# Causal attention of 16 heads: f32 matmuls replaced by three float32r products of split operands, with operands split on ScalarE, VectorE and GpSimd

## The chip, the cores and the metric

The kernel runs on one core of a Trainium2 chip. The metric is the device time of one execution in microseconds (us), measured without a profile; below it stands the time of before. The core has a matrix engine, TensorE (PE, with its weight loads shown apart as PEld), and VectorE (DVE), ScalarE (ACT), GpSimd (POOL) and SyncE (SP), which issues DMA. The engines run by themselves and meet at semaphores; each carries out its own instructions strictly in the order in which they are written.

## The reference

The program is a stack of 16 layers over one stream x of 1024 tokens with 256 features. The change is in one of them, the first attention of the third block ("L2a"):

```python
x = x + _L2_attn_a_ref(_layernorm(x, axis=-1), L2_attn_a_W_Q, L2_attn_a_W_K, L2_attn_a_W_V, L2_attn_a_W_O)

q = jnp.einsum('bsd,hed->bhse', x, W_Q)
scores = jnp.einsum('bhse,bhme->bhsm', q, k) * scale
scores = jnp.where(causal, jnp.float32(-1000000000.0), scores)
pattern = jax.nn.softmax(scores, axis=-1)
z = jnp.einsum('bhsm,bhme->bhse', pattern, v)
out = jnp.einsum('bhse,hde->bsd', z, W_O)
```

## The kernel before

All tensors of the layer are f32. `hT` holds the normalised x with features on the partitions. For each of the 16 heads `wide_attention` projects q and k (each [128, 1024], as two halves of 512 tokens: the items q0, k0, q1, k1) and v (items v0, v1), computes the scores of 8 tiles of 128 query rows, takes the row maximum, exponentiates, turns the probabilities with PE against an identity, multiplies by v, and projects with Wo into x.

The work is laid out by hand. A head has 8 slots s, one for each row tile, in the order `ROW_ORDER = (3, 7, 2, 6, 1, 5, 0, 4)`; row tile t sees t+1 key tiles, so the widths are 512, 1024, 384, 896, 256, 768, 128 and 640 columns. In slot s of head p, PE computes the scores of row s (`score`), then what `BESIDE[s]` lists, then the turn of the row before (`turn`). `BESIDE` places the six projections of head p+1 ("make0" to "make5") and, for head p-1, the products with v ("sum0", "sum1", for the lower and the upper 512 tokens) and the four pieces of the output projection ("y0" to "y3"):

```python
BESIDE = (("make0", "sum0"), ("make1", "y0"), ("make2", "sum1"), ("y1",), ("y2",), ("make3", "y3"), ("make4",), ("make5",))
```

The makes, sums and y pieces share two PSUM banks in turn. `wait_shared` lets PE write a bank only when the item two places before it has been taken out: semaphore `kept` for a make, `out_kept` for a sum, `y_added` for a y. The scores have two pairs of banks, the turned probabilities have one pair (`ps_turn`): PE turns a row into it only when the row before has been taken out (`first_kept` for the first four key tiles, `second_kept` for the rest).

The other engines repeat the slots in the same order. DVE: `find_max` of row s (L2173), `keep_second` of row s-1 (L2183), then beside it `keep_out` for a sum (L2191) and `add` for a y (two instructions on L2204). ACT: `exp` of row s (L2139), which waits for the maximum; `keep_made` for a make (L2123 q, L2125 k, L2127 v); `keep_first` of row s-1 (L2147). The PE lines are L2009 (q and k), L2014 (v), L2026 (scores), L2028 (mask), L2039 (turn), L2057 (sums) and L2069 (y). Of the helpers, `products` and `multiply_parts` (L130) are used before the change by the feed-forward layers alone; they give each product of two split operands as high*high, high*low and low*high.

Of the kernel before, what the change touches and what calls it, by code (L numbers as in the profile page):

```python
# [14 lines left out]
P = 128  # L15
TOK = 1024
D = 256
# [1884 lines left out]
MADE = ("q0", "k0", "q1", "k1", "v0", "v1")  # L1902

# [3 lines left out]

def shared_uses(heads):

    uses = [("make", 0, n) for n in range(len(MADE))]  # L1910
    for p in range(heads):
        for slot in BESIDE:
            for item in slot:
                kind, n = item[:-1], int(item[-1])
                h = p + 1 if kind == "make" else p - 1
                if 0 <= h < heads:
                    uses.append((kind, h, n))
# [3 lines left out]
def wide_attention(core, name, w, heads, scale):  # L1921

    nc, x, hT = core.nc, core.x, core.hT
    NM = len(MADE)
    uses = shared_uses(heads)
    place = {use: r for r, use in enumerate(uses)}
    column = [ROW_ORDER.index(t) for t in range(NT)]
    with Stage(core, name) as st:
        following = core.next.open(st)
        block = st.opened  # L1930
        wo = st.sb("wo", [P, heads, D])
        q, k = [st.sb(f"q{n}", [P, TOK]) for n in range(2)], [st.sb(f"k{n}", [P, TOK]) for n in range(2)]
        v = [st.sb(f"v{n}", [P, NT, P]) for n in range(2)]
        probs = [st.sb(f"probs{n}", [P, TOK]) for n in range(2)]
        probsT = [[st.sb(f"probsT{n}_{half}", [P, 4 * half + 4, HALF]) for half in range(2)] for n in range(2)]
        outT = [st.sb(f"outT{half}", [P, HALF]) for half in range(2)]
# [10 lines left out]
        wo_in, made, kept = st.sem("wo_in"), st.sem("made"), st.sem("kept")  # L1947
        scored, maxed, exped = st.sem("scored"), st.sem("maxed"), st.sem("exped")
        first_turned, second_turned = st.sem("first_turned"), st.sem("second_turned")
        first_kept, second_kept = st.sem("first_kept"), st.sem("second_kept")  # L1950
        summed, out_kept, inverted = st.sem("summed"), st.sem("out_kept"), st.sem("inverted")
# [10 lines left out]
        def wait_shared(engine, kind, h, n):  # L1962

            r = place[kind, h, n]
            if r >= 4:
                kind, h, n = uses[r - 2]
                if kind == "make":
                    engine.wait_ge(kept, h * NM + n + 1)
# [5 lines left out]
        def beside(p, s):  # L1974
            for item in BESIDE[s]:
                kind, n = item[:-1], int(item[-1])
                h = p + 1 if kind == "make" else p - 1
                if 0 <= h < heads:
                    yield kind, h, n

# [4 lines left out]
        def _(sp):  # L1985
            sp.dma_start(wo[:], core.dram[f"{name}_wo"]).then_inc(wo_in, 16)
# [7 lines left out]
        def _(pool):  # L1994
            st.clear_old(pool)
            for g in range(NT):
# [2016 lines left out]
```

## Time and profile before

| | us |
|---|---|
| time, median of 3 runs (2952.99 to 2956.48) | 2955.17 |
| time of the profiled execution | 2954.47 |
| its span in the profile | 2952.7 |
| PE busy in the span | 2796.7 |
| DVE busy | 1606.9 |
| ACT busy | 1324.7 |
| POOL busy | 613.0 |
| the heads of L2a, first row maximum to last | 1388.26 to 1922.09 |

The profiled execution lies 0.7 us below the median of the runs, and 1.8 us of it lie outside the span. The busy times are sums over 16 layers of different kinds. PE is busy for 95% of the span. The layer of the change takes about 545 us of it, from 1379 to about 1925 us, and its 16 heads repeat the same pattern.

### The profile page before, as it was taken

The numbers are of one execution on the slowest core, as the hardware profiler recorded it, in microseconds if no ns is written. First come the engines' busy times: TensorE is split into PE (matmuls) and PEld (weight loads), VectorE is DVE, ScalarE is ACT, GpSimd is POOL, SyncE is SP. The second block draws the span as 40 slices with busy tenths as digits, with TensorE's granted clock in tenths as the row PEclk, the third lists the DMA queues.
The fourth block names the chain that finished last, engine by engine and source line by source line (L and its number), as shares of the span: only waits on it lengthen the run. The fifth ranks groups of instructions, "written<-read, shape, count | busy, mean of one in ns | idle before, by whom it ended". The sixth has DMA issues, their size and how long they took to land. (4 is left out here: it accounts for less than half of the span.)

```text
span 2952.7 us, 44166 instructions
## 1 busy us (share of the span) xinstructions
PE 2796.7 (95%) x16121; PEld 1871.8 (63%) x16121; DVE 1606.9 (54%) x3495; ACT 1324.7 (45%) x2711; POOL 613.0 (21%) x737
## 2 busy tenths in 40 slices
PE   7989998999999998999999999989999999989979
PEld 4454475644676886887666666666666667754545
DVE  7758545687346666664333333454333332478587
ACT  3745634547443333334334343344343433336576
POOL 2021002030013331432000000013333331130185
PEclk9999999999999999999999999999999999999989
DMA  3021010030103321531000000000000000121031
GB/s 98 21 61 55 10 43 28 1 88 2 53 12 103 112 81 39 148 110 51 11 11 17 12 11 24 1 33 11 17 13 16 17 35 13 40 52 38 13 97 55
DMA packets 69378, 122.17 MB, mean 41 GB/s; under 512 B 15791, under 2 KB 44817, under 8 KB 68897
## 3 DMA queue, kind: packets, MB, share of 16 engines
q1 hardware_dynamic: 67564, 118.04, 13.6%
q8 instruction: 131, 2.15, 0.3%
q10 hardware_dynamic: 1600, 1.31, 0.3%
q14 instruction: 83, 0.67, 0.1%
HBM read 92.21 MB, written 1.54 MB: 32 GB/s over the span
## 5 line engine op out<-in xcount | busy, mean ns | idle before, releaser
L236 POOL TENSOR_TENSOR scale<-scale,powers 128x1 f32<-128x1 f32 (+1 forms) x98 | 57.4, 586 | 1382.3 <-DVE scale L217 1382.3
L130 PE MATMUL psum<-L1f_hT_part,L1f_wide 128*128 128x512 f32 x1104 | 271.7, 396 | 6.1 <-DVE L1f_inner L2561 5.5
L130 PEld LDWEIGHTS psum<-L1f_hT_part,L1f_wide 128*128 128x128 f32 x1104 | 203.8, 190 | 50.8 <-DVE L1f_inner L2561 9.6
L1702 ACT ACTIVATE L2b_tanh<-psum,L2b_inverse 128x512 f32<-128x512 f32 x192 | 110.6, 579 | 269.7 <-PE psum L1650 268.3
L1281 ACT ACTIVATE L0f_weights<-psum 128x512 f32<-128x512 f32 (+2 forms) x320 | 157.0, 566 | 95.5 <-PE psum L1097 75.2
L2369 POOL TENSOR_TENSOR L1f_inner<-L1f_inner,L1f_weight 128x512 f32<-128x512 f32 x96 | 143.1, 1500 | 268.0 <-DVE L1f_inner L2561 177.6
L130 PE MATMUL psum<-L1f_down,L1f_inner_part 128*128 128x256 f32 x1152 | 159.7, 291 | 16.1 <-DVE L1f_inner_part L2577 16.1
L2139 ACT ACTIVATE L2a_probs<-psum,L2a_negmax 128x512 f32<-128x512 f32 (+7 forms) x128 | 95.0, 742 | 173.8 <-DVE L2a_negmax L2173 173.7
L130 PEld LDWEIGHTS psum<-L1f_down,L1f_inner_part 128*128 128x128 f32 x1152 | 154.1, 198 | 25.0 <-DVE L1f_inner_part L2577 19.4
L1659 PEld LDWEIGHTS psum<-L2b_v,L2b_weights 128*128 128x128 f32 x1152 | 141.3, 193 | 40.2 <-issue 28.7
L2183 DVE COPY L2a_probsT<-psum 128x512 f32<-128x512 f32 (+1 forms) x64 | 31.4, 491 | 228.5 <-PE psum L2039 228.5
L2500 ACT ACTIVATE L1f_gate<-psum 128x512 f32<-128x512 f32 x96 | 57.4, 598 | 217.3 <-PE psum L130 188.4
L1650 PE MATMUL psum<-L2b_q,L2b_k 128*128 128x512 f32 (+3 forms) x384 | 149.9, 487 | 1.0 <-DVE L2b_q L1768 0.8
L1659 PE MATMUL psum<-L2b_v,L2b_weights 128*128 128x129 f32 x1152 | 145.2, 278 | 5.8 <-POOL L2b_weights L1568 5.8
L2577 DVE TENSOR_TENSOR L1f_inner_part<-L1f_inner,L1f_inner_part 128x512 fp32r<-128x512 f32 x96 | 142.3, 1491 | 10.5 <-ACT L1f_inner_part L2521 10.5
L2026 PE MATMUL psum<-L2a_k,L2a_q 128*128 128x512 f32 (+3 forms) x384 | 146.3, 490 | 0.0
L2173 DVE TENSOR_REDUCE L2a_negmax<-psum 128x1 f32<-128x512 f32 (+7 forms) x128 | 96.6, 755 | 82.7 <-PE psum L2028 82.6
L2057 PE MATMUL psum<-L2a_probsT,L2a_v 128*128 128x512 f32 (+3 forms) x384 | 129.4, 486 | 0.3 <-DVEq L2211 0.3
L1063 PE MATMUL psum<-L0f_ks,L0f_qs 96*128 96x512 bf16 (+3 forms) x384 | 111.5, 332 | 9.9 <-DVE L0f_piece_max L1362 5.6
L2009 PE MATMUL psum<-hT,L2a_early 128*128 128x512 f32 x248 | 119.8, 606 | 0.7 <-PEq L103 0.7
L2147 ACT COPY L2a_probsT<-psum 128x512 f32<-128x512 f32 (+3 forms) x128 | 64.7, 505 | 124.1 <-PE psum L2039 122.3
L2561 DVE TENSOR_TENSOR L1f_inner<-psum,L1f_gate 128x512 f32<-128x512 f32 x96 | 66.0, 689 | 97.6 <-ACT L1f_gate L2500 94.0
(555 smaller groups left out, 6274.5 us busy)
## 6 DMA issues: line engine op xcount, KB each, us to landing
L1f_w<-in_L1f_w SPq DMA_DIRECT2D x32, 384.0 KB, 3.9
L1f_weight<-combine SPq DMA_DIRECT2D x32, 384.0 KB, 4.3
L1f_weight<-combine SPq DMA_DIRECT2D x32, 256.0 KB, 4.8
scan_spread_b<-bc SPq DMA_DIRECT2D x16, 512.0 KB, 3.7
L0f_qs<-L0f_part SPq DMA_DIRECT2D x96, 64.0 KB, 2.6
experts_early<-in_L1f_w SPq DMA_DIRECT2D x16, 384.0 KB, 4.3
L2a_early<-in_L2a_w SPq DMA_DIRECT2D x16, 384.0 KB, 3.0
L2b_early<-in_L2b_w SPq DMA_DIRECT2D x16, 384.0 KB, 3.0
```

Of the source, the lines that this page charges most:

```text
L130: last = nc.tensor.matmul(to, stationary, moving, start=start and n == 0, stop=stop and n == len(pairs) - 1, skip_group_check=skip)
L1063: last = nc.tensor.matmul(to[:, a:b], qs[0:SPLIT, half, h, i * P:(i + 1) * P], ks[0:SPLIT, kh, h, 0:width], start=True, stop=not masks)
L1281: nc.scalar.activation(to, src, ACT.Exp, scale=HD ** -0.5).then_inc(exped, 1)
L1650: nc.tensor.matmul(ps_scores[u % 3][:, at:], k[e][:, kt * P:(kt + 1) * P], q[e][:, half * HALF + at:(half + 1) * HALF], start=True, stop=T ...
L1659: last = nc.tensor.matmul(ps_out[t % 2][:, 0:P + 1], weights[UNITS.index((kt, t // 4))][:, at:at + P], v[e][:, kt, :], start=(kt == 0), st ...
L1702: nc.scalar.activation(tanhs[u % 3][:, at:], ps_scores[u % 3][:, at:], ACT.Tanh, scale=inverse[e][:, NT + kt:NT + kt + 1]).then_inc(capped, 1)
L2009: last = nc.tensor.matmul(to[:], w[h % 2][:, c, at:at + P], hT[:, c, half * HALF:(half + 1) * HALF], start=(c == 0), stop=(c == DC - 1))
L2026: nc.tensor.matmul(ps_scores[i % 2][:, a:b], q[h % 2][:, t * P:(t + 1) * P], k[h % 2][:, a:b], start=True, stop=b < width(i))
L2057: last = nc.tensor.matmul(to[:, at:], v[h % 2][:, kt, :], probsT[h % 2][half][:, kt, at:], start=(kt == 0), stop=(kt == tiles - 1))
L2173: nc.vector.tensor_reduce(negmax[:, i:i + 1], ps_scores[i % 2][:, 0:width(i)], AX, ALU.max, negate=True).then_inc(maxed, 1)
L2369: nc.gpsimd.tensor_tensor(inner[u % INNER][:], inner[u % INNER][:], weight[n % SPREAD][:, half * HALF:(half + 1) * HALF], ALU.mult).then_i ...
L2577: nc.vector.tensor_tensor(low[:], inner[u % INNER][:], high[:], ALU.subtract).then_inc(inner_low, 1)
```

## The change

Every product of the layer but the q and k projections of head 0 is computed as three float32r matmuls. For this each operand X becomes two float32r tensors, high = X rounded and low = X - high. ACT writes the high part of what comes out of PSUM (q, k, v, turned probabilities, sums) and DVE then reads the same PSUM bank again and writes the low part; only then does the bank come free (`kept`, `first_kept`, `second_kept` and `out_kept` are now counted by DVE). POOL splits the weights, which were used as they came before. ACT and DVE split `hT` ahead of the first head. The values are projected for two heads at once (256 columns), in four items of two token tiles: v0 to v3 ahead of head 0, and after that two of four in each head. The turned probabilities, double-buffered before, have one buffer, the row's probabilities lie in `h`, and Wo is loaded head by head. The core of the diff:

```diff
-            for h in range(2, heads):
-                sp.wait_ge(made, (h - 1) * NM)
-                sp.dma_start(w[h % 2][:], core.dram[f"{name}_w"][h]).then_inc(w_in[h % 2], 16)
...
+            def part(whole, parts, done):
+                high, low = parts
+                nc.gpsimd.tensor_copy(high[:], whole[:]).then_inc(part_high, 1)
+                split[0] += 1
+                pool.wait_ge(part_high, split[0])
+                nc.gpsimd.tensor_tensor(low[:], whole[:], high[:], ALU.subtract).then_inc(done, 1)
...
+                        pairs = []
+                        for c in range(DC):
+                            pairs += products([part[:, c, t * P:(t + 1) * P] for part in hT_parts],
+                                              [part[:, c, :] for part in wv_parts[j % 2]])
+                        last = multiply_parts(nc, to[:, e * D:(e + 1) * D], pairs, start=True, stop=True)
...
-                    nc.tensor.matmul(ps_scores[i % 2][:, a:b], q[h % 2][:, t * P:(t + 1) * P], k[h % 2][:, a:b],
-                                     start=True, stop=b < width(i))
+                    multiply_parts(nc, ps_scores[i % 2][:, a:b],
+                                   products([part[:, t * P:(t + 1) * P] for part in q[h % 2]],
+                                            [part[:, a:b] for part in k[h % 2]]),
+                                   start=True, stop=b < width(i))
...
-            def keep_first(h, i):
+            def keep_turned(h, i):
                 act.wait_ge(first_turned, h * NT + i + 1)
-                if h >= 2 and i < 2:
-                    act.wait_ge(summed, 2 * (h - 2) + i + 1)
+                if h and i < 2:
+                    act.wait_ge(summed, 2 * (h - 1) + i + 1)
...
+            def keep_out(h, half):
+                act.wait_ge(summed, 2 * h + half + 1)
+                if h:
+                    act.wait_ge(y_ready, 4 * h - 2 + 2 * half)
+                nc.scalar.copy(outT[half][0][:], shared_bank("sum", h, half)[:]).then_inc(out_high, 1)
...
+            def keep_made(h, n):
+                kind = FIRST_MADE[n][0]
+                dve.wait_ge(made_high, makes[h, n] + 1)
...
+                nc.vector.scalar_tensor_tensor(low, src[:], scale if kind == "q" else 1.0, high, ALU.mult, ALU.subtract
+                                               ).then_inc(kept, 1)
...
+            def keep_turned(h, i):
+                dve.wait_ge(first_high, h * NT + i + 1)
+                t, tiles = ROW_ORDER[i], min(width(i) // P, 4)
+                tokens = slice(t % 4 * P, (t % 4 + 1) * P)
+                high, low = (part[:, 0:tiles, tokens] for part in probsT[t // 4])
+                nc.vector.tensor_tensor(low, ps_turn[0][:, 0:tiles * P].rearrange("p (k t) -> p k t", k=tiles), high,
+                                        ALU.subtract).then_inc(first_kept, 1)
...
             for p in range(heads):
                 for s in range(NT):
                     find_max(p, s)
                     if s or p:
-                        keep_second(p - (s == 0), (s - 1) % NT)
+                        keep_turned(p - (s == 0), (s - 1) % NT)
                     if s == 1 and p:
                         invert(p - 1)
                     for kind, h, n in beside(p, s):
-                        if kind == "sum":
+                        if kind == "make":
+                            keep_made(h, n)
+                        elif kind == "sum":
                             keep_out(h, n)
```

The diff does not show at once how this moves the queues. DVE's queue before, from the maximum that opens slot 1 of a head in the middle of the layer to the one that opens slot 3 (L2173 is `find_max`, L2195 `invert`, L2183 `keep_second`, L2191 `keep_out`, L2204 `add`):

```order
L2173 TENSOR_REDUCE L2a_negmax<-psum 128x1
L2195 RECIPROCAL L2a_inverse<-L2a_row_sum 128x8
L2204 SCALAR_TENSOR_TENSOR x<-psum,L2a_inverse,x 128x256 x2
L2173 TENSOR_REDUCE L2a_negmax<-psum 128x1
L2183 COPY L2a_probsT_1<-psum 128x4x128
L2191 COPY L2a_outT<-psum 128x512
L2173 TENSOR_REDUCE L2a_negmax<-psum 128x1
```

Between two maxima stood two or three other instructions, and those that wait, wait for PE. DVE's queue now, from the maximum that opens slot 1 to the one that opens slot 3 (L2308 is `find_max`, L2333 `invert`, L2316 and L2322 `keep_turned`, L2302 `keep_made`, L2328 `keep_out`, L2342 `add`):

```order
L2308 TENSOR_REDUCE L2a_negmax<-psum 128x1
L2316 TENSOR_TENSOR L2a_probsT_1<-psum,L2a_probsT_0 128x4x128
L2333 RECIPROCAL L2a_inverse<-L2a_row_sum 128x8
L2302 SCALAR_TENSOR_TENSOR L2a_k_1<-psum,L2a_k_0 128x512
L2342 SCALAR_TENSOR_TENSOR x<-psum,L2a_inverse,x 128x256 x2
L2308 TENSOR_REDUCE L2a_negmax<-psum 128x1
L2316 TENSOR_TENSOR L2a_probsT_1<-psum,L2a_probsT_0 128x4x128
L2322 TENSOR_TENSOR L2a_probsT_1<-psum,L2a_probsT_0 128x4x128
L2302 SCALAR_TENSOR_TENSOR L2a_q_1<-psum,L2a_q_0 128x512
L2328 TENSOR_TENSOR L2a_outT_1<-psum,L2a_outT_0 128x512
L2308 TENSOR_REDUCE L2a_negmax<-psum 128x1
```

Between the maxima of two slots there are now four or five instructions (the `add` is two), and the first of them, L2316, waits for ACT's copy of the row before. ACT's queue before, from the exponential of slot 0 to that of slot 3 (L2139 is `exp`, L2123 and L2125 `keep_made`, L2147 `keep_first`):

```order
L2139 ACTIVATE L2a_probs,L2a_row_sum<-psum,L2a_negmax 128x512
L2123 ACTIVATE L2a_q<-psum 128x512
L2147 COPY L2a_probsT_1<-psum 128x4x128
L2139 ACTIVATE L2a_probs,L2a_row_sum<-psum,L2a_negmax 128x1024
L2125 COPY L2a_k<-psum 128x512
L2147 COPY L2a_probsT_0<-psum 128x4x128
L2139 ACTIVATE L2a_probs,L2a_row_sum<-psum,L2a_negmax 128x384
L2123 ACTIVATE L2a_q<-psum 128x512
L2147 COPY L2a_probsT_1<-psum 128x4x128
L2139 ACTIVATE L2a_probs,L2a_row_sum<-psum,L2a_negmax 128x896
```

Each slot held one exponential, at most one projection and one turned copy. ACT's queue now, from slot 0 to the copy of the sum in slot 2 (L2237 is `exp`, L2224 and L2226 `keep_made`, L2260 `keep_out`, L2246 and L2252 `keep_turned`):

```order
L2237 ACTIVATE h,L2a_row_sum<-psum,L2a_negmax 128x512
L2224 ACTIVATE L2a_q_0<-psum 128x512
L2260 CAST L2a_outT_0<-psum 128x512
L2246 CAST L2a_probsT_0<-psum 128x4x128
L2252 CAST L2a_probsT_0<-psum 128x128
L2237 ACTIVATE h,L2a_row_sum<-psum,L2a_negmax 128x1024
L2226 CAST L2a_k_0<-psum 128x512
L2246 CAST L2a_probsT_0<-psum 128x4x128
L2237 ACTIVATE h,L2a_row_sum<-psum,L2a_negmax 128x384
L2224 ACTIVATE L2a_q_0<-psum 128x512
L2260 CAST L2a_outT_0<-psum 128x512
```

The copy of the turned row (L2246) still stands behind the exponential of its slot, which waits for the maximum of that slot on DVE, and now also behind the copy of a sum (L2260), which waits for PE.

## Rows read from the trace of the kernel before

**Rows 1.** Head of the page: span, busy time and count of PE.
```profile
span 2952.7 us, 44166 instructions
...
PE 2796.7 (95%) x16121; PEld 1871.8 (63%) x16121; DVE 1606.9 (54%) x3495; ACT 1324.7 (45%) x2711; POOL 613.0 (21%) x737
```

**Rows 2.** Busy time by window: first head, two heads, two short stretches.
```profile
core 0: us, PE busy (x) PEld busy (x) DVE busy (x) ACT busy (x) POOL busy (x), PEclk, DMA share, GB/s
...
1388.26:1414.45 26.19, 24.24 (x112) 15.33 (x112) 7.64 (x11) 13.58 (x30) 0.00 (x0) 0.93 0.05 16
1414.45:1448.98 34.53, 34.41 (x157) 22.12 (x157) 12.47 (x23) 13.61 (x30) 0.00 (x0) 1.00 0.05 13
...
1398.49:1401.90 3.41, 1.46 (x11) 0.95 (x9) 1.42 (x2) 1.85 (x5) 0.00 (x0) 1.00 0.00 0
1401.90:1405.31 3.41, 3.41 (x11) 2.22 (x10) 0.56 (x1) 0.67 (x2) 0.00 (x0) 0.50 0.00 0
```

**Rows 3.** Who waited for whom while the heads of this layer ran.
```profile
engine line waited for: us in total, times, longest us
DVE L2a_probsT L2183 <- PE psum L2039: 226.5, 63, 7.7
ACT L2a_probs L2139 <- DVE L2a_negmax L2173: 172.1, 106, 3.5
```

**Rows 4.** Timeline of PE in three places: start, length, merged count.
```profile
899.28 1.39 PE L2447 MATMUL psum<-experts_early,hT 128*128 128x32 f32 x11 [0.42 <-PEq L103]
...
1249.76 1.60 PE L130 MATMUL psum<-L1f_down,L1f_inner_part 128*128 128x256 f32 x12
1251.19 2.91 PE L130 MATMUL psum<-L1f_hT_part,L1f_wide 128*128 128x512 f32 x12
...
1395.00 1.45 PE L2009 MATMUL psum<-hT,L2a_early 128*128 128x512 f32 x3
```

**Rows 5.** Groups of the page: row maxima, exponentials, first copies of this layer.
```profile
L2139 ACT ACTIVATE L2a_probs<-psum,L2a_negmax 128x512 f32<-128x512 f32 (+7 forms) x128 | 95.0, 742 | 173.8 <-DVE L2a_negmax L2173 173.7
...
L2173 DVE TENSOR_REDUCE L2a_negmax<-psum 128x1 f32<-128x512 f32 (+7 forms) x128 | 96.6, 755 | 82.7 <-PE psum L2028 82.6
...
L2147 ACT COPY L2a_probsT<-psum 128x512 f32<-128x512 f32 (+3 forms) x128 | 64.7, 505 | 124.1 <-PE psum L2039 122.3
```

**Rows 6.** Groups with their shapes kept apart, VectorE and then ScalarE.
```profile
L2561 DVE TENSOR_TENSOR L1f_inner<-psum,L1f_gate 128x512 f32<-128x512 f32 x96 | 66.0, 689 | 97.6 <-ACT L1f_gate L2500 94.0 <-PE psum L130 3.0 <-issue 0.5
L2204 DVE SCALAR_TENSOR_TENSOR x<-psum,L2a_inverse,x 128x256 f32<-128x256 f32 x128 | 55.8, 477 | 44.2 <-PE psum L2069 44.1
...
L2557 DVE SCALAR_TENSOR_TENSOR L2f_inner<-psum,L2f_w,L2f_gate 128x512 f32<-128x512 f32 x16 | 12.0, 751 | 26.3 <-ACT L2f_gate L2500 26.3
L2183 DVE COPY L2a_probsT<-psum 128x512 f32<-128x512 f32 x16 | 11.1, 692 | 115.4 <-PE psum L2039 115.4
...
L2183 DVE COPY L2a_probsT<-psum 128x384 f32<-128x384 f32 x16 | 8.9, 558 | 25.7 <-PE psum L2039 25.7
...
L2183 DVE COPY L2a_probsT<-psum 128x256 f32<-128x256 f32 x16 | 6.8, 425 | 30.3 <-PE psum L2039 30.3
...
L2183 DVE COPY L2a_probsT<-psum 128x128 f32<-128x128 f32 x16 | 4.7, 292 | 57.1 <-PE psum L2039 57.1
...
L2127 ACT COPY L2a_v<-psum 128x512 f32<-128x512 f32 x32 | 18.7, 586 | 15.6 <-PE psum L2014 14.2
```

**Rows 7.** Timeline of VectorE and ScalarE in two places.
```profile
1391.80 1.23 DVE L2173 TENSOR_REDUCE L2a_negmax<-psum 128x1 f32<-128x1024 f32 x1 [2.85 <-PE psum L2028]
...
1393.06 1.11 ACT L2139 ACTIVATE L2a_probs<-psum,L2a_negmax 128x1024 f32<-128x1024 f32 x1 [2.44 <-DVE L2a_negmax L2173]
...
1504.35 0.86 DVE L2204 SCALAR_TENSOR_TENSOR x<-psum,L2a_inverse,x 128x256 f32<-128x256 f32 x2
```

**Rows 8.** Groups with their shapes kept apart: one of VectorE, one of GpSimd.
```profile
L2577 DVE TENSOR_TENSOR L1f_inner_part<-L1f_inner,L1f_inner_part 128x512 fp32r<-128x512 f32 x96 | 142.3, 1491 | 10.5 <-ACT L1f_inner_part L2521 10.5
...
L2369 POOL TENSOR_TENSOR L1f_inner<-L1f_inner,L1f_weight 128x512 f32<-128x512 f32 x96 | 143.1, 1500 | 268.0 <-DVE L1f_inner L2561 177.6 <-DMA L1f_weight<-combine 90.4
```

More of the change, by code:

```diff
@@ L1967, in wait_shared @@
                 if kind == "make":
[L1968 removed]
+                    engine.wait_ge(kept, makes[h, n] + 1)
                 elif kind == "sum":
@@ L1977, in beside, with last_of_values @@
                 h = p + 1 if kind == "make" else p - 1
-                if 0 <= h < heads:
+                if 0 <= h < heads and (kind != "make" or n < made_of(h, heads)):
                     yield kind, h, n
+        def last_of_values(j):
+            return makes[(0, 7) if j == 0 else (2 * j, 5)]
         def free_bank(g):
@@ L2020, in score @@
                 if i == 0:
-                    pe.wait_ge(kept, h * NM + 4)
+                    pe.wait_ge(kept, makes[h, 3] + 1)
                 if h * NT + i >= 2:
@@ L2056, in add_values @@
                     at = max(kt - 4 * half, 0) * P
-                    last = nc.tensor.matmul(to[:, at:], v[h % 2][:, kt, :], probsT[h % 2][half][:, kt, at:],
-                                            start=(kt == 0), stop=(kt == tiles - 1))
+                    last = multiply_parts(nc, to[:, at:],
+                                          products([part[:, kt, h % 2 * P:(h % 2 + 1) * P] for part in v[h // 2 % 2]],
+                                                   [part[:, kt, at:] for part in probsT[half]]),
+                                          start=(kt == 0), stop=(kt == tiles - 1))
                 last.then_inc(summed, 1)
             def project(h, n):
-                if h == 0 and n == 0:
-                    pe.wait_ge(wo_in, 16)
+                if n == 0:
+                    pe.wait_ge(wo_parted, h + 1)
                 pe.wait_ge(out_kept, 2 * h + n // 2 + 1)
@@ L2068, in project @@
                     at = (2 * n + e) % 4 * P
-                    last = nc.tensor.matmul(to[:, e * D:(e + 1) * D], outT[n // 2][:, at:at + P], wo[:, h, :],
-                                            start=True, stop=True)
+                    last = multiply_parts(nc, to[:, e * D:(e + 1) * D],
+                                          products([part[:, at:at + P] for part in outT[n // 2]],
+                                                   [part[:] for part in wo_parts[h % 2]]), start=True, stop=True)
                 last.then_inc(y_ready, 1)
@@ L2076, in turn_next @@
                 following.turn(nc.tensor, g, free_bank(g))
-            for n in range(NM):
+            for n in range(len(FIRST_MADE)):
                 if (n, 0) in begun:
@@ L3911, in attention_weights, with head_weights @@
     return np.stack(out)
+def head_weights(wq, wk, wv):
+    heads = wq.shape[1] // P
+    qk = [rows_in_chunks(np.concatenate([w[:, h * P:(h + 1) * P] for w in (wq, wk)], 1)) for h in range(heads)]
+    v = [rows_in_chunks(wv[:, 2 * j * P:2 * (j + 1) * P]) for j in range(heads // 2)]
+    return np.stack(qk), np.stack(v)
 def quad_columns(w):
```

211 lines of the change are left out of this document (156 added, 55 removed).

## The prediction

> **What bounds the kernel now.** I read the head of the page first: PE is busy for 2796.7 of 2952.7 us [rows 1]. That is an average over 16 layers, so I went to the windows of the changed one. Each head after the first takes 34.53 us, and in it PE is busy 34.41, DVE 12.47 and ACT 13.61 us [rows 2]: PE sets the pace and the others have more than half their time free. The waits say the same from the other side: DVE and ACT wait for PE or for one another, 226.5 us in the longest entry [rows 3]. The reader should carry two things further: PE's work of a head, and the time around the loop in which DVE and ACT serve a slot, which is hidden behind PE today.
>
> **PE's work, which the change cuts.** A record's length minus the last one's tail gives PE's pitch. An f32 matmul is two records; of 512 columns (1.45 - 0.59)/2 = 0.43 us each, 0.86 for the product. A float32r product is one record: (2.91 - 0.40)/11 = 0.228 us for 512 columns, (1.60 - 0.28)/11 = 0.120 for 256 [rows 4], so about 0.174 for 384. Three of 512 cost 0.68 against 0.86. No float32r product of 128 columns is in the trace. The line through 512 and 256 gives 0.067; an f32 record of only 32 columns still takes (1.39 - 0.28)/10 = 0.111 [rows 4], which I read as the floor of a weight load of this type; four times the float32r rate of the 512 columns would be 0.228. I take 0.111 and keep 0.067 and 0.228 as bounds. Per head now: q and k 24 x 0.228 = 5.5 us; v 24 x 0.120 = 2.9; scores and sums each 18 x 0.228 + 6 x 0.174 + 6 x 0.120 + 6 x 0.111 = 6.5, together 13.0; y 24 x 0.120 = 2.9; the 36 turns and 8 masks are unchanged, 4.3 (my estimate: 36 x 0.11 and 8 x 0.05). The sum is 28.6 us, 5.9 less than now.
>
> **The loop of DVE and ACT, which the change lengthens.** In one slot DVE finds the maximum, ACT waits for it and exponentiates, then copies the high parts (a projection, a sum, last the turned row), DVE waits for that last copy and writes the low parts, adds a y, and only then comes to the next maximum. Both queues are strictly in order, so these pieces follow one another and never lie side by side, whatever PE does. The loop of a head is therefore at least their sum:
>
> DVE maxima 96.6/16 = 6.0 and ACT exponentials 95.0/16 = 5.9 [rows 5]. ACT high parts: six projections at 0.59 = 3.5, two sums 1.2 (L2127) [rows 6], turned rows 64.7/16 = 4.0 [rows 5]. DVE low parts, which read one operand from PSUM and one from SBUF as L2561 does (0.689 for 512 columns [rows 6]; its copies cost the same): turned rows, first part 5 x 0.69 + 0.56 + 0.43 + 0.29 = 4.7 and second part 0.69 + 0.56 + 0.43 + 0.29 = 2.0; q and k four at 0.75 (L2557), v two at 0.69, 4.4; sums two at 0.69, 1.4; eight adds at 0.477 = 3.8 [rows 6]. Together 36.9. ACT's second copies of turned rows run beside DVE's first low part and cost nothing. A hand-over between DVE and ACT costs 1393.06 - (1391.80 + 1.23) = 0.03 us [rows 7]; three in each of 8 slots are 0.8. Two DVE instructions without a wait between them overlap by 2 x 0.477 - 0.86 = 0.09 [rows 6, 7]; of the 36 of a head 28 follow so, -2.4. The loop takes 35.3 us at least.
>
> That is already more than the 34.53 of now, so the cut in PE's work can't be collected. And PE's pieces enter the loop where ACT or PE waits:
> - Slot 2: PE may write make2 into its bank only after DVE wrote the low part of make1. Then come make2 (1.37), sum1 (15 products of 512, three each of 384, 256, 128: 4.6), a tail of 0.17 and two hand-overs, 6.3 us, until ACT copies the sum. Without PE the loop would need 2.5 for the same way (adds 0.9, maximum and exponential of the 384-wide row 1.1, start of the copies 0.5). Adds 3.8.
> - Slot 0: sum0 waits for the low part of make5; 1.9 + 0.2 us against 1.8 of the loop. Adds 0.3.
> - Slot 6: make4 waits for the low part of make3, and row 5 is turned only behind it: 1.44 + 0.44 + 0.2 + the hand-over against 2.0. Adds 0.3.
>
> So a head takes 35.3 + 4.4 = 39.7 us, against 34.53: +5.2, over 14 of the 15 intervals between first rows 73 us. Taking PE's waits from my reading of the queues is the choice here; with none of them the sum is 35.3.
>
> **The ends of the layer.** Start: ACT copies four pieces of hT (4 x 0.6 = 2.4) before it takes out any projection, and the values of two heads come before the first scores, 48 x 0.120 = 5.8 us where 3.6 was; +5 with the low parts. First head: no sums beside it, +2. Last head: ACT's copy and DVE's low part in line for each sum, 2 x 0.6, and the loop's excess with no projections beside it, about +5 in all. SP's loads become smaller and more, 16 Wo pieces among them; they have a whole head each, and I cost them at nothing. POOL does two instructions for the weights, two for Wo and on average one for the values in a head. Even at 1.5 us each (L2369) [rows 8] they are 7.5 of 40 us and a head ahead of their use: nothing. If this cover were gone PE would wait for `w_parted`.
>
> **TensorE's clock.** PE will stand idle 2.2 to 2.5 us at a time, four or five times a head. The trace shows what that can do: with PE busy only 1.46 of 3.41 us the granted clock was 1.00, and in the next 3.41 us it was 0.50, the lower of the two levels [rows 2]. In such a stretch PE's pieces take twice as long; it costs the loop something where those pieces are in it, 10.5 of 40 us. I estimate 25 such stretches in the layer at 0.8 us each, +20; bounds 0 and 40.
> The Trainium skill ("TensorE: Matmul & The Clock Gate", the section on HAM oscillation) says that a kernel whose PE idles again and again between groups of matmuls keeps falling to the half clock, and puts the loss at half of the throttled time. The fall in [rows 2] agrees. Its loss for 25 stretches would be 43 us, and the time 3082; I stay lower because much of PE's work has slack here.
>
> **Sum.** 73 + 5 + 2 + 5 + 20 = 105. The profiled execution took 2954.5 us, so 3059.5; it lies 0.7 below the median, so 3060.
>
> **The rivals.**
> - *PE stays the bound* (the other side). If low parts overlapped with the rest, a head would take 28.6 us: 15 x -5.9 and a few for the ends, 2872. For it speaks only that DVE and ACT have 20 us of a head free. It needs the loop below 34.5, that is its instructions 15% shorter than their rows, with PE's pieces still 4.4 outside. Chance 0.05.
> - *The loop without PE's waits.* 35.3 a head: 15 x 0.8 and 12 for the ends, 2979. The waits on banks would have to be met in time; against it stands that sum1 alone is 4.6 us in the middle of a loop slot of 5.5. Chance 0.10.
> - *Slower still.* The clock falls twice as often (+20), and a 128-column product costs 0.228: six such products of the sums and six of the scores, of which the former are in the loop, +0.7 a head, +11. With some instruction issue for the many double waits, 3095. Chance 0.22.
> - *Nothing to be seen*: gain and loss cancel, which no term here makes; 0.02.
>
> **How the numbers follow.** The forecast has 0.61, so the time is 3060. Its own range is 3030 to 3085. The 8-in-10 range takes in the slower rival and part of the way to the loop alone: 3005 to 3115. What a measurement can tell from no change is about 0.2%, 6 us: faster 0.05, same 0.02, slower 0.93.
>
> **What the profile after would show.** Windows of one head: near 40 us, PE busy about 29 to 33, DVE about 22, ACT about 19 to 20. Waits: PE for DVE's low parts (`kept`, `first_kept`), over 100 us in the layer; DVE's first low part for ACT's copy, over 200 us. Between consecutive maxima of a head DVE and ACT take turns. The timeline of PE gives the 128-column product. PEclk in the slices of this layer below 1.0. I would be wrong if the 0.689 us of L2561 doesn't hold for a subtraction that writes float32r into strided rows, if the queues overlap where I put them in line, or if the clock stays full.

## The result, and the profile after

The changed kernel takes 3055.56 us (median of 4 runs, 3054.02 to 3056.93) against 2955.11 for the kernel before (4 runs, 2952.99 to 2956.48): a ratio of 1.0341, interval 1.0324 to 1.0357. It is 100 us slower; 3060 was forecast. The profiled execution took 3054.63 us. The head of its page answers to [rows 1]:

```profile
span 3052.9 us, 45708 instructions
...
PE 2768.9 (91%) x16625; PEld 1963.6 (64%) x16625; DVE 1728.0 (57%) x3723; ACT 1358.3 (44%) x2811; POOL 676.1 (22%) x815
```

PE is busy for 27.8 us less and the span is 100.2 us longer, so PE no longer sets the pace. The busy times by window are the partners of [rows 2]: two heads in the middle of the layer, two stretches of half a slot, and all heads from the first row maximum to that of head 15's last row.

```profile
core 0: us, PE busy (x) PEld busy (x) DVE busy (x) ACT busy (x) POOL busy (x), PEclk, DMA share, GB/s
1508.53:1549.20 40.67, 33.20 (x190) 28.69 (x189) 19.70 (x38) 15.47 (x36) 2.96 (x4) 0.92 0.06 17
1549.20:1589.37 40.17, 32.37 (x191) 27.58 (x189) 19.61 (x38) 15.38 (x36) 4.78 (x6) 0.96 0.04 11
1535.66:1539.08 3.42, 1.52 (x12) 1.42 (x12) 1.61 (x4) 1.74 (x4) 2.96 (x4) 1.00 0.03 7
1539.08:1545.91 6.83, 6.13 (x26) 5.84 (x27) 3.25 (x8) 1.91 (x5) 0.00 (x0) 0.50 0.31 96
1397.71:2024.86 627.15, 504.21 (x2866) 430.12 (x2864) 303.56 (x571) 241.24 (x562) 51.75 (x68) 0.93 0.04 12
```

A head takes 40.67 us where it took 34.53. No engine is busy all of it. DVE and ACT have 35.2 us of work between them, and by the starts and lengths of their instructions only 1.2 of it lie side by side: they take turns. For the other 6.7 us of the head both stand idle. In the third line PE worked 1.52 of 3.42 us at the full clock; behind it stand 6.83 us at half. In the last line the stretches at half clock add up to 92 us, 27 of 3.4 us each; between the same two maxima the kernel before had one.

The waits of the same stretch answer to [rows 3]:

```profile
engine line waited for: us in total, times, longest us
...
DVE L2a_probsT L2316 <- ACT L2a_probsT L2246: 320.7, 126, 7.8
ACT h L2237 <- DVE L2a_negmax L2308: 291.2, 126, 3.1
...
ACT L2a_outT L2260 <- PE psum L130: 71.5, 30, 5.5
PEld psum L130 <- DVE L2a_k L2302: 57.6, 27, 2.2
PE psum L130 <- DVE L2a_k L2302: 53.9, 27, 2.1
```

The first two lines are the loop: DVE waits 126 times for ACT's copy of a turned row, ACT waits 126 times for DVE's maximum. They are the two links of one ring. The last three are where PE enters it. One such passage, slot 2 of a head, on the timeline of the kernel after (start, length, merged count, idle time before in brackets; the weight loads are left out):

```profile
1518.24 0.64 DVE L2302 SCALAR_TENSOR_TENSOR L2a_k<-psum,L2a_k 128x512 fp32r<-128x512 f32 x1
...
1518.94 1.64 PE L130 MATMUL psum<-L2a_hT_part,L2a_w_part 128*128 128x512 f32 x6 [1.92 <-DVE L2a_k L2302]
1519.58 0.55 DVE L2308 TENSOR_REDUCE L2a_negmax<-psum 128x1 f32<-128x384 f32 x1
1520.17 0.58 ACT L2237 ACTIVATE h<-psum,L2a_negmax 128x384 f32<-128x384 f32 x1 [2.67 <-DVE L2a_negmax L2308]
...
1520.42 4.74 PE L130 MATMUL psum<-L2a_probsT,L2a_v 128*128 128x512 f32 x24
...
1525.19 0.59 ACT L2260 CAST L2a_outT<-psum 128x512 fp32r<-128x512 f32 x1 [3.87 <-PE psum L130]
1525.67 0.59 ACT L2246 CAST L2a_probsT<-psum 128x512 fp32r<-128x512 f32 x1
...
1526.30 0.69 DVE L2316 TENSOR_TENSOR L2a_probsT<-psum,L2a_probsT 128x512 fp32r<-128x512 f32 x1 [6.17 <-ACT L2a_probsT L2246]
```

From the end of DVE's low part (1518.88) to ACT's copy of the sum (1525.19) are 6.31 us, and DVE stands still for 6.17 of the slot. That is the passage of "slot 2" in the prediction, with its 6.3 us.

Groups of the kernel after with their shapes kept apart give the prices of the new instructions, for which rows of [rows 6] stood in before. The first group covers the heads, the last the start of the layer:

```profile
L2316 DVE TENSOR_TENSOR L2a_probsT<-psum,L2a_probsT 128x512 fp32r<-128x512 f32 x79 | 54.6, 692 | 244.2 <-ACT L2a_probsT L2246 244.2
...
L2302 DVE SCALAR_TENSOR_TENSOR L2a_q<-psum,L2a_q 128x512 fp32r<-128x512 f32 x30 | 20.4, 680 | 1.3 <-ACT L2a_q L2224 1.3
L2328 DVE TENSOR_TENSOR L2a_outT<-psum,L2a_outT 128x512 fp32r<-128x512 f32 x30 | 20.4, 679 | 0.0
L2302 DVE SCALAR_TENSOR_TENSOR L2a_k<-psum,L2a_k 128x512 fp32r<-128x512 f32 x30 | 19.8, 661 | 0.0
...
L2359 DVE TENSOR_TENSOR L2a_hT_part<-hT,L2a_hT_part 128x512 fp32r<-128x512 f32 x4 | 5.2, 1360 | 2.9 <-ACT L2a_hT_part L2265 2.9
```

A low part of 512 columns costs 0.69 us, as its stand-in did. The last line is twice that, and is taken up below. The product of 128 columns, which no row before showed, stands at the end of a sum, on the timeline of PE:

```profile
1524.59 0.57 PE L130 MATMUL psum<-L2a_probsT,L2a_v 128*128 128x256 f32 x4
1524.99 0.30 PE L2128 MATMUL psum<-ident,h 128*128 128x128 f32 x1
```

The row holds one product of 256 columns (0.12) and three of 128; the next begins 0.40 us behind its start, so the three take 0.28. The start of the next record follows 0.058 us behind the first and 0.11 behind the second and third: the 0.111 read from the 32-column record in [rows 4] holds for two of the three.

**Where the 100 us are.** From the layer's first projection (1380.06 before, 1381.34 after) to the first row maximum 8.20 us became 16.37: +8.2. The first interval between heads went from 26.19 to 28.31: +2.1. The 14 that follow went from 34.53 to 40.70 on average: +86.4. From the first maximum of head 15 to the next layer's first product 44.70 became 51.05: +6.4. The sum is +103.1; the rest of the program gives 2.9 back (the layer begins 1.3 later, and what follows it is 4.2 shorter), which isn't explained here.

### The profile page after: what moved, and what is told of

It is laid out like the page before. It is cut to its first block and busy times, and to the rows that moved or that the text cites. A ratio compares the mean times of both kernels' runs of the same rounds, so it can differ in the third digit from the quotient of the medians.

```text
span 3052.9 us, 45708 instructions
## 1 busy us (share of the span) xinstructions
PE 2768.9 (91%) x16625; PEld 1963.6 (64%) x16625; DVE 1728.0 (57%) x3723; ACT 1358.3 (44%) x2811; POOL 676.1 (22%) x815
## 5 line engine op out<-in xcount | busy, mean ns | idle before, releaser
L2316 DVE TENSOR_TENSOR L2a_probsT<-psum,L2a_probsT 128x512 fp32r<-128x512 f32 (+3 forms) x128 | 75.7, 591 | 323.7 <-ACT L2a_probsT L2246 323.7
L236 POOL TENSOR_TENSOR scale<-scale,powers 128x1 f32<-128x1 f32 (+1 forms) x98 | 57.6, 588 | 870.1 <-DVE scale L217 870.1
L2237 ACT ACTIVATE h<-psum,L2a_negmax 128x512 f32<-128x512 f32 (+7 forms) x128 | 95.0, 742 | 292.8 <-DVE L2a_negmax L2308 292.8
L130 PE MATMUL psum<-L2a_hT_part,L2a_w_part 128*128 128x512 f32 x360 | 103.3, 424 | 36.0 <-DVE L2a_k L2302 26.9
L130 PE MATMUL psum<-L2a_probsT,L2a_v 128*128 128x512 f32 (+3 forms) x576 | 119.0, 363 | 6.4 <-DVE L2a_v L2296 4.7
L130 PEld LDWEIGHTS psum<-L2a_probsT,L2a_v 128*128 128x128 f32 x576 | 105.5, 203 | 26.1 <-DVE L2a_v L2296 7.5
L2128 PE MATMUL psum<-ident,h 128*128 128x128 f32 x576 | 91.3, 289 | 33.0 <-DVE L2a_probsT L2316 32.9
```

The costliest lines, as they stand in the source:

```text
L130: last = nc.tensor.matmul(to, stationary, moving, start=start and n == 0, stop=stop and n == len(pairs) - 1, skip_group_check=skip)
L2128: last = nc.tensor.transpose(ps_turn[c // 4][:, c % 4 * P:(c % 4 + 1) * P], probs[i % 2][:, c * P:(c + 1) * P], core.ident[:])
L2237: nc.scalar.activation(probs[i % 2][:, 0:width(i)], ps_scores[i % 2][:, 0:width(i)], ACT.Exp, bias=negmax[:, i:i + 1], accum_out=row_sum[h ...
L2316: nc.vector.tensor_tensor(low, ps_turn[0][:, 0:tiles * P].rearrange("p (k t) -> p k t", k=tiles), high, ALU.subtract).then_inc(first_kept, 1)
```

## Experiments

The theory on trial is the prediction's: the strictly ordered queues of DVE and ACT form one loop, longer than PE's work, into which some of PE's pieces fall, and the clock falls behind PE's waits. Against it stand PE's own work, the count of added instructions, and the clock as the main cause. Differences between kernels are between medians, where nothing else is said.

**1. DVE's low part of the turned row moved to the end of its slot** (ratio 0.9934, interval 0.9917 to 0.9951).

```diff
                     find_max(p, s)
-                    if s or p:
-                        keep_turned(p - (s == 0), (s - 1) % NT)
                     if s == 1 and p:
                         invert(p - 1)
                     for kind, h, n in beside(p, s):
...
                             add(h, n)
+                    if s or p:
+                        keep_turned(p - (s == 0), (s - 1) % NT)
```

> The changed kernel with one thing moved: in each slot VectorE writes the low parts of the turned row last, behind the low parts of projections and sums and the adds, where it wrote them first. Nothing is computed otherwise. Theory of the loop: the low parts of projections and sums and the adds then lie beside the exponential and the copies of ScalarE, and the loop of a head falls from about 40 us to about 33, near PE's own work of 28 to 29; the time is about 2935 (2920 to 2955), 120 less than with the change as it was. Rival, the amount of work: if VectorE's and ScalarE's added work or PE's lower clock set the time, and not the order of the queues, the same instructions take the same time, 3050 to 3056. Rival, the two shared banks: if PE's waits for the banks are the cause in themselves, a bank still needs a high and a low part, and only part of the 40 goes, 3010 or so.

It took 2934.90 us (2931.14 to 2937.64), 120.7 less than the kernel after, with the same instructions in another order. One head by window, and its waits over 500 us of the layer:

```profile
1491.39:1524.03 32.64, 29.98 (x190) 25.97 (x188) 19.88 (x38) 15.34 (x36) 2.96 (x4) 1.00 0.07 21
```

```profile
ACT h L2237 <- DVE L2a_negmax L2308: 209.1, 124, 2.1
...
DVE L2a_probsT L2316 <- ACT L2a_probsT L2246: 21.8, 35, 1.5
```

DVE is as busy as before the move (19.88 against 19.70), so it isn't the count of its instructions. Its wait for the turned copy has gone from 320.7 us to a few dozen. Now DVE takes out a projection while ACT copies the turned row, and DVE + ACT exceed the head (35.2 against 32.64): 5.4 us of them lie side by side, where it was 1.2. That the order of the queues sets the loop is shown here; what the clock has to do with it is told by experiment 2.

**2. Every y product carried out twice** (1.0276, 1.0258 to 1.0295). More work for PE, in the places where it mostly idles.

```diff
-                    last = multiply_parts(nc, to[:, e * D:(e + 1) * D],
-                                          products([part[:, at:at + P] for part in outT[n // 2]],
-                                                   [part[:] for part in wo_parts[h % 2]]), start=True, stop=True)
+                    for _ in range(2):
+                        last = multiply_parts(nc, to[:, e * D:(e + 1) * D],
+                                              products([part[:, at:at + P] for part in outT[n // 2]],
+                                                       [part[:] for part in wo_parts[h % 2]]), start=True, stop=True)
```

> The changed kernel with PE's products of the output projection computed twice (the second overwrites the first with the same values): 24 more products of 256 columns in a head, 2.9 us, 46 us over the layer. Theory of the loop with a cost of the clock: PE's added work lies in its idle time; at full clock it would cost 0.3 us a head, 5 us, and PE idles less, so the clock falls less often, which gives back 3 to 8: 3050 to 3057. The loop without a cost of the clock: 3060. Rival, PE is the bound: 3095 to 3102.

3037.07 us (3029.94 to 3039.86): 18.5 less than the kernel after, with 384 products more. One head and the heads together:

```profile
1509.91:1549.03 39.12, 33.41 (x212) 28.88 (x212) 19.62 (x39) 15.50 (x36) 3.02 (x4) 1.00 0.06 18
1403.27:2005.39 602.12, 510.81 (x3226) 441.35 (x3224) 303.27 (x571) 241.53 (x562) 52.66 (x68) 0.99 0.04 12
```

The granted clock was 1.00 in this head and 0.99 over all, with 6.8 us at half between the first and the last maximum instead of 92. So the loop at full clock takes at most 39.1 us, with the doubled products in it, and the half clock costs the kernel after at least 40.70 - 39.12 = 1.6 us a head. The expectation of 3050 to 3057 was missed: it had the better clock give back 3 to 8 us, and by the heads it was 22 at least. It isn't the main cause even so: 39.1 is still 4.6 over the 34.53 of before.

**3. No low parts of q and k** (1.0161, 1.0144 to 1.0178). DVE's low parts of q and k are cut to one column each, and the scores multiply the high parts three times, so the scores leave the low parts out and PE's work stays.

```diff
-                                   products([part[:, t * P:(t + 1) * P] for part in q[h % 2]],
-                                            [part[:, a:b] for part in k[h % 2]]),
+                                   products([q[h % 2][0][:, t * P:(t + 1) * P]] * 2,
+                                            [k[h % 2][0][:, a:b]] * 2),
```

> The changed kernel without the low parts of q and k: VectorE writes one column of each in place of 512, and the scores take the high part in all three products, so PE does the same number of them on other values, and the output is another. Theory of the loop: four pieces of 0.68 less 0.06, with their overlap of 0.09 some 2.3 us, go out of the loop of each head: 37 us, and up to 8 more since the shared banks come free earlier in slots 0 and 2: 3010 to 3020. Rival, PE or its clock sets the time: 3050 to 3056, since PE's work is the same.

3001.86 us (2998.12 to 3004.14), 53.7 less than the kernel after, and 8 below the range expected. One head:

```profile
1463.31:1499.97 36.66, 30.68 (x188) 26.04 (x188) 17.58 (x38) 15.40 (x36) 4.79 (x6) 1.00 0.04 12
```

DVE does 2.1 us less in this head, and the head is 4.0 shorter than 40.67 (others take up to 38.5). Part of that is a better clock, 41 us at half instead of 92. The head of experiment 2, 39.12, tells the two apart, since both had the full clock: against it this one is 2.5 shorter, with 2.0 less of DVE's work. So instructions of DVE count in the loop in full.

**4. Only the projections as split products, on the kernel before** (0.9903, 0.9887 to 0.992). q, k and v of this kernel are plain f32 tensors, written by ACT alone; scores, sums and y stay f32, and so do all queues around the maxima. Of the change it has `part` on POOL, the split of `hT`, the values of two heads at once and these lines of `make`:

```diff
+                        for c in range(DC):
+                            pairs += products([part[:, c, t * P:(t + 1) * P] for part in hT_parts],
+                                              [part[:, c, :] for part in wv_parts[j % 2]])
+                        last = multiply_parts(nc, to[:, e * D:(e + 1) * D], pairs, start=True, stop=True)
```

> One part of the change alone, on the kernel before: only the projections of q, k (heads 1 to 15) and v are computed as three float32r products, v for two heads at once, with hT split by ScalarE and VectorE and the weights by GpSimd. q, k, v, the probabilities and the sums stay f32 with one copy each, and scores, sums and output projection stay f32 products. PE's work of a head falls by 16 x 0.43 - 24 x 0.228 = 1.4 us for q and k and 32 x 0.111 - 24 x 0.120 = 0.7 for v, and the loop of VectorE and ScalarE stays at about 26 us, so PE sets the pace: 15 x 2.1 = 31 us less and 3 more for the start, about 2927 (2918 to 2935). If float32r products brought nothing here for a reason of PE itself (its waits, its clock), it would be 2950 to 2960.

2925.33 us (2923.03 to 2927.24), 27.7 less than its own reference of 2953.00. One head:

```profile
1483.85:1516.34 32.49, 32.37 (x157) 22.87 (x157) 12.46 (x23) 13.34 (x30) 1.90 (x2) 1.00 0.03 9
```

PE is still busy all the time and its saving of 2.0 us a head is collected. The cheaper products are worth what their records say wherever PE is the bound; POOL's splits, the loads and the joined values cost nothing to be seen in a head. So the split products don't slow the kernel by themselves; what slows it lies in what DVE and ACT have to do for low parts of q, k, v, turned rows and sums, which this kernel hasn't.

**5. ACT copies the turned row right behind the exponential** (1.0201, 1.0184 to 1.0218). The same idea as experiment 1 on the other side of the hand-over.

```diff
                     exp(p, s)
+                    if s or p:
+                        keep_turned(p - (s == 0), (s - 1) % NT)
                     for kind, h, n in beside(p, s):
...
                             keep_out(h, n)
-                    if s or p:
-                        keep_turned(p - (s == 0), (s - 1) % NT)
```

> The changed kernel with one thing moved on ScalarE: in each slot it copies the turned row right behind the exponential, ahead of the copies of projections and sums; VectorE's order is that of the change. Theory of the loop: VectorE's first low part waits for a copy that now comes earlier, except in slots where PE turns the row late, so the copies of projections and sums lie beside VectorE's low parts. Walking the queues with the durations of the rows gives some 1.5 us less a head: about 3031 (3015 to 3042). Rival, the amount of work: no change, 3050 to 3056.

3013.33 us (3012.22 to 3015.38), 42.2 less than the kernel after and 18 less than expected, just below the range. Heads took 37.7 to 39.5 us, with 26 us at half clock. DVE gets what it waits for earlier, at a third of the gain of experiment 1: 4.8 us of a head now lie side by side, nearly as much as there, but both engines are idle for 7.3 us of it.

**6. Both moves** (1.0286, 1.0269 to 1.0303): the diffs of 1 and 5 in one kernel.

> The changed kernel with both moves: ScalarE copies the turned row ahead of projections and sums, and VectorE writes its low part behind theirs. Each move alone takes something out of the loop; together they put the longest way back in, since VectorE now waits first for ScalarE's last copy and only then serves the turned row that ScalarE copied first, and PE's next turn waits for that. Theory of the loop: worse than with neither, about 3080 (3062 to 3098), 145 more than with VectorE's move alone. Rival, that each move helps by itself (less waiting wherever the work is spread out): 2910 to 2940. Rival, the amount of work: 3050 to 3056.

3039.88 us (3036.51 to 3041.58). Each move alone helps, and together they lose 105 us against the first alone. The expectation had it near 3080, slower than with neither move, and that was wrong: it is 15.7 us faster than the kernel after. What held is that the second move spoils the first. Slot 2 of a head on the timeline of this kernel:

```profile
1523.14 0.59 ACT L2246 CAST L2a_probsT<-psum 128x512 fp32r<-128x512 f32 x1 [5.83 <-PE psum L2128]
...
1524.10 0.61 ACT L2224 ACTIVATE L2a_q<-psum 128x512 fp32r<-128x512 f32 x1
...
1524.75 0.69 DVE L2302 SCALAR_TENSOR_TENSOR L2a_q<-psum,L2a_q 128x512 fp32r<-128x512 f32 x1 [8.15 <-ACT L2a_q L2224]
```

and the same slot with only DVE's part moved (experiment 1):

```profile
1501.87 0.59 ACT L2224 ACTIVATE L2a_q<-psum 128x512 fp32r<-128x512 f32 x1
1502.49 0.69 DVE L2302 SCALAR_TENSOR_TENSOR L2a_q<-psum,L2a_q 128x512 fp32r<-128x512 f32 x1 [1.23 <-ACT L2a_q L2224]
```

With both moved, ACT waits 5.83 us for a turn that stands behind a whole sum in PE's queue, and the copy of q that DVE wants first waits behind it: DVE stands still for 8.15 us instead of 1.23. (1.6 of that is the clock, at half in a part of this slot: in a head at full clock it is 6.55. With only DVE's part moved it waits again behind q, for the sum, for 3.2.) My reading is that both queues should take the items in an order in which the one asks for what the other has just done.

**7. Another table, nothing else** (1.0178, 1.0161 to 1.0195). It parts sum1 from make2, so that the long sum begins a slot, with a slot's scores behind it, and spreads the rest.

```diff
-BESIDE = (("make0", "sum0"), ("make1", "y0"), ("make2", "sum1"), ("y1",), ("y2",), ("make3", "y3"), ("make4",), ("make5",))
+BESIDE = (("make0",), ("sum0",), ("sum1", "y0"), ("y1", "make1"), ("make2", "make3"), ("y2",), ("make4", "make5"), ("y3",))
```

> The changed kernel with another table BESIDE and nothing else: make0; sum0; sum1, y0; y1, make1; make2, make3; y2; make4, make5; y3. The second sum no longer follows make2, which waited for the low part of make1, and the projections come later. Theory of the loop: all of VectorE's and ScalarE's work stays in line, but PE's pieces leave the loop in slot 2, some 3 us a head: about 3006 (2995 to 3020). Rival, that the line of work by itself sets the time and PE's pieces in it are of no account: 3040 to 3056.

3006.59 us (3004.44 to 3009.48), 49 less than the kernel after; heads of 36.4 to 38.0 us. Two of them, one after the other:

```profile
1466.03:1502.45 36.42, 30.25 (x190) 26.13 (x189) 19.62 (x39) 15.45 (x36) 3.94 (x6) 1.00 0.07 19
1502.45:1540.45 38.00, 31.84 (x190) 27.24 (x189) 19.61 (x38) 15.45 (x36) 3.98 (x5) 0.96 0.03 11
```

The second has one stretch of 3.4 us at half clock, and it is 1.6 us longer: that is what the clock costs here. The first has none, and against the 39.12 of experiment 2, with the same work of DVE and ACT and still only 1.2 us of it side by side, it is 2.7 us shorter. So of the 4.4 us of PE's pieces that the prediction put into the loop this table takes out 2.7. Over the heads DVE still waits for the turned copy:

```profile
DVE L2a_probsT L2316 <- ACT L2a_probsT L2246: 268.4, 123, 4.9
```

**8. The late low part and the new table together** (0.9772, 0.9756 to 0.9788).

> The changed kernel with VectorE's low parts of the turned row moved last in the slot and the table BESIDE of the run named spread. Theory of the loop: both pieces gone, PE's own 28 us a head is nearly the bound, 29.3 a head against 32.6 with the move alone: about 2891 (2878 to 2905), faster than the kernel before and than its projections alone in float32r. Rival, that the amount of VectorE's work (20 us busy of 32.6) or PE's weight loads (26 of 32.6) is the next bound: 2925 to 2940.

2887.94 us (2883.79 to 2889.30), 67.5 less than the kernel before and 167.6 less than the kernel after. One head:

```profile
1482.56:1511.82 29.26, 29.26 (x190) 25.77 (x189) 19.77 (x39) 15.45 (x36) 4.37 (x6) 1.00 0.05 14
```

PE is busy for all of it: the head has reached PE's work, 29.26 us where the prediction had summed 28.6. Between the first and the last maximum the granted clock never falls, without any work added for it. With the same instructions as the kernel after, only the order in which they stand decides between +3.4% and -2.3%.

**9. GpSimd begins its splits only when `hT` has been split**, on the kernel of experiment 8, in one execution.

```diff
+            pool.wait_ge(hT_low, 2 * DC)
             part_values(0)
             part_heads(1)
```

> The kernel of the run late_spread, with GpSimd's first split of weights held back until VectorE has written the low parts of hT. In late_spread these four subtractions of 512 columns (two operands in SBUF) took 5.22 us in all while GpSimd split weights. If GpSimd slows them, they take about 0.69 us each here, 2.8 in all, and the first product of the values starts some 2.4 us earlier after the layer's first product. If they are slow for their own sake, they stay at 1.3 us and the values start later, by what GpSimd now does late. The time itself, one look, changes by less than can be told: 2880 to 2893.

It took 2879.43 us, and the kernel before 2951.08 beside it; with one execution a few us are not to be told apart, so the trace has to speak. DVE's low parts of `hT`, four merged, first in experiment 8 and then here:

```profile
1383.10 5.22 DVE L2359 TENSOR_TENSOR L2a_hT_part<-hT,L2a_hT_part 128x512 fp32r<-128x512 f32 x4 [2.94 <-ACT L2a_hT_part L2265]
```

```profile
1380.71 2.50 DVE L2360 TENSOR_TENSOR L2a_hT_part<-hT,L2a_hT_part 128x512 fp32r<-128x512 f32 x4 [2.95 <-ACT L2a_hT_part L2266]
```

They take 2.50 us instead of 5.22, and the first product of the values begins 4.99 us behind the layer's first projection instead of 7.39: 2.4 us sooner. From there to the first row maximum, again experiment 8 and then experiment 9:

```profile
1390.17:1399.17 9.00, 9.00 (x55) 8.43 (x56) 3.23 (x5) 2.97 (x5) 2.86 (x4) 0.81 0.24 80
1385.39:1392.87 7.48, 7.48 (x55) 6.92 (x56) 2.90 (x6) 2.98 (x5) 6.49 (x8) 1.00 0.28 88
```

The same 55 products take 1.5 us less, at a granted clock of 1.00 instead of 0.81: behind PE's shorter wait the clock didn't fall. In all the start is 3.9 us shorter. With one execution of this kernel it isn't shown that the fall stays away each time.

**What the order changes.** In every kernel of the table below DVE and ACT have 35 us of work a head. A head is that work, less what lies side by side, plus the time in which both are idle. From the starts and lengths of the instructions, a head each, all at full clock but the first:

| kernel | a head, us | side by side | both idle |
|---|---|---|---|
| after (6.8 us at half clock) | 40.67 | 1.2 | 6.7 |
| 2, y products twice | 39.12 | 1.2 | 5.2 |
| 1, DVE's low part late | 32.64 | 5.4 | 2.8 |
| 5, ACT's copy early | 37.73 | 4.8 | 7.3 |
| 6, both moves | 38.79 | 2.8 | 6.4 |
| 7, other table | 36.42 | 1.2 | 2.5 |
| 8, low part late, other table | 29.26 | 7.6 | 1.6 |

DVE's move gains at both, ACT's move gains side by side and loses in idle time, and the other table gains idle time alone. Idle time of both is what the loop's hand-overs and PE's pieces cost.

## Why the prediction was right, and which terms were off

**The bound.** "The cut in PE's work can't be collected" held: the loop of DVE and ACT set the head. Experiment 1 shows the loop, experiment 4 that the cut in PE's work is real where PE is the bound, experiment 8 that both are there at once. The rival "PE stays the bound" (2872) needed exactly the order of experiment 8, which reached 2888; for the change as it was written it had no case. Its condition in the prediction, a loop below 34.5, was too weak besides: that would only have made the change no loss, and 28.6 a head needs a loop of 28.6.

**PE's work.** 28.6 us a head was forecast and 29.26 measured, with PE busy throughout (experiment 8); which term is short isn't shown. The product of 128 columns is near the 0.111 taken: three in a row take 0.28 us, 0.05 less than 3 x 0.111. The bounds 0.067 and 0.228 weren't reached.

**The loop a head.** 39.7 us at full clock was forecast; experiment 2 puts it at 39.1 or less. One term is mis-sized for certain: the low parts of q and k cost 0.68 and 0.66, not 0.75, 0.3 us a head. The sum splits into DVE's and ACT's work in line, 36.9 - 2.4 = 34.5, and time in which both are idle, 0.8 of hand-overs and 4.4 of PE's pieces, 5.2. In experiment 2 at least one of them works for 33.9 us of a head, and both are idle for 5.2, with what the doubled products add. So the time for PE held, slot 2 with its 6.3 us in it, and the 0.6 that are missing lie in the work. The shown busy times: PE 32 to 33 (29 to 33 said), DVE 19.7 (about 22 said) and ACT 15.4 (19 to 20 said). The last two were slips of mine: 22 is the sum of DVE's lengths without the overlap of 2.4, which the loop's sum had taken off, and the terms for ACT add up to 14.6 and its second copies, not to 19. The sum itself didn't use them.

**The clock.** +20 us in 25 stretches of 3.4 us was forecast, which is 85 us at half clock; the 14 intervals have 85 at half, which is 25 stretches, and by experiment 2 they cost at least 1.6 us a head, 22 in all. At the 1.6 us a stretch of experiment 7 it would be 40 (an estimate; in experiment 5 one stretch costs as little as 0.7). So the count of the falls was right and the 0.8 us of each too low, and the loop without them lies, by this estimate and experiment 2, between 37.8 and 39.1 us. The two terms of the 14 intervals, 73 for a loop taken too long and 20 for a clock taken too cheap, make 93 against the 86.4 measured.
The Trainium skill ("TensorE: Matmul & The Clock Gate", the section on HAM oscillation) counts half of the throttled time as lost. For the 85 us that is 43, an estimate by that page. The 1.6 us for 3.4 at half clock in experiment 7 are close to it, nearer than my 0.8; the 0.7 in experiment 5 are not. Experiment 2 excludes that the clock explains the slowdown, since even the kernel without most of it is 84 us slower than the kernel before beside it.

**The ends.** First head +2 (2.1 measured) and last head +5 (6.4) held. The start was +8.2 instead of +5. The step that failed there is "POOL ... nothing": POOL's splits of the weights fall on DVE's low parts of `hT`, which then take 1.36 us instead of about 0.65. Experiment 9 gave 3.9 us back, 2.4 by the subtractions and 1.5 by the clock, which had fallen behind PE's wait for them. That leaves +4.3 where +5 was said.

**How near the sum came.** Forecast were 93 for the 14 intervals and 12 for the start, the first and the last head; measured were 86.4 and 16.7, and 2.9 came back elsewhere. The mechanism held, but that the total is off by only 5 us owes something to luck: its errors go both ways.

**The rivals.** *The loop without PE's waits* (2979) fell: PE's wait in slot 2 is in the trace. *Slower still* (3095) asked for twice as many falls of the clock and 0.228 for 128 columns; neither came, though a fall may cost twice what it was put at. *Nothing to be seen* fell.

**The shows.** PE's waits for DVE's low parts of k alone are 53.9 us by the matmuls and 57.6 by the weight loads, which stand for nearly the same waits; with q (22.8), v (4.7) and the turned rows (30.7), which `kept` and `first_kept` take in, they are 112 by the matmuls, "over 100" said. DVE's wait for ACT is 320.7 us, "over 200" said. The clock over the heads is 0.93.

## What to carry to other kernels

Before work is moved from one engine to others, write down the ring of instructions through which two in-order queues hand over to one another, and add it up: an engine that is busy for less than half of the time (19.7 of 40.67 us here) can already be the end of the road, when every instruction it gets lies in line with the other's. Then order each queue so that what an engine asks for first is what its partner has just finished, and keep long pieces of a third engine out of the slots in which both wait; change one queue and look before changing its partner too, since two moves that help alone can undo one another's gain. And a queue that idles in short pieces pays twice, by the wait and by the clock behind it.

## What the hardware showed that I had not expected

More work made a kernel faster: with 384 products added (experiment 2) the time fell by 18.5 us, as the granted clock over the heads rose from 0.93 to 0.99.

GpSimd and VectorE slow one another. Beside GpSimd's splits DVE's subtraction of two SBUF operands took 1.36 us for 512 columns, and alone 2.50 us for four. The second and third instruction of GpSimd's splits in the same two kernels, experiment 8 and then experiment 9:

```profile
1383.49 1.60 POOL L2040 TENSOR_TENSOR L2a_wv_part<-L2a_early,L2a_wv_part 128x512 fp32r<-128x512 f32 x1
1385.03 1.07 POOL L2037 CAST L2a_w_part<-L2a_early 128x512 fp32r<-128x512 f32 x1
```

```profile
1383.97 1.27 POOL L2040 TENSOR_TENSOR L2a_wv_part<-L2a_early,L2a_wv_part 128x512 fp32r<-128x512 f32 x1
1385.18 0.62 POOL L2037 CAST L2a_w_part<-L2a_early 128x512 fp32r<-128x512 f32 x1
```

GpSimd's subtraction takes 1.60 instead of 1.27 us and its cast 1.07 instead of 0.62, so both sides lose. In experiment 8 itself the next subtraction of GpSimd that begins behind the last of DVE's takes 1.27 again. DVE's low parts out of PSUM, one SBUF operand each, kept their 0.68 us beside the same GpSimd instructions.
The Trainium skill ("GPSIMD Engine Reference", the section on key points) says that GpSimd contends with VectorE instructions that have two SBUF inputs. The runs agree, and the 1491 ns of a subtraction with two SBUF operands in [rows 8], double the 0.69 of one, were a row in which I could have seen it.
